# Last stage of a transformer layer: weight rows one chunk further ahead on GpSimd and ScalarE, and the residual of half of the tiles added on VectorE

## The chip, the cores and the metric

The kernel runs on one core of a Trainium2 chip. Times are device microseconds (us) of one execution. The core has five engines that run their own instruction streams side by side: TensorE (PE, with its weight loads as PEld), VectorE (DVE), ScalarE (ACT), GpSimd (POOL) and SyncE (SP, which here issues transfers). They are tied together by semaphores alone: an instruction may wait until a counter has reached a number, and may raise a counter when it is done.

## The reference, cut to what matters

One layer over 32 x 256 = 8192 tokens of width 128: windowed attention with 16 heads, residual and layer norm, then a mixture of 8 experts of which each token takes two, residual and layer norm. The change lies in the very last part:

```
combine = zeros((t, e)).at[arange(t)[:, None], top_idx].add(top_w)
y   = einsum('tef,efd->ted', h, w2) + b2
out = einsum('ted,te->td', y, combine)         # two weighted rows per token
x   = _layernorm(x + out, axis=-1)             # (x - mean) / sqrt(var + 1e-5)
```

So each token's result is the layer norm of residual + w0 * z0 + w1 * z1, where z0 and z1 are the rows that its two experts gave.

## The kernel before

Three stages follow one another: attention with the routing (its last score matmul starts at 387.3 us), the experts (71 steps of 256 tokens; their last scatter is issued at 694.5 us), and the last stage, which begins when the last expert rows have been scattered to the DRAM tensor zs and takes the rest. Only this last stage is touched.

It works through 64 tiles of 128 tokens in 16 chunks of 4 tiles (`CHUNKS = 16`, `CH = 4`). For chunk c:

- SP loads both expert rows of its tokens (512 KB) from zs into one of 6 buffers of `zin` (line 567). The load of chunk c+6 waits for the sum of chunk c, and stands in SP's order behind the store of chunk c-1.
- POOL multiplies the second rows by their weights, one instruction of 128x512 (line 654). I call it z1(c).
- ACT multiplies the first rows of the first two tiles (`ZA = 2`, line 815), z0a(c). DVE does the last two (line 1143), z0b(c).
- PE adds up in one PSUM bank of four (`total(c)`), each time with the identity as weights: the residual Y (line 1375), z1 (line 1377), z0 (line 1380). PE waits for z1(c), z0a(c) and z0b(c), and for the output of chunk c-4, whose bank it takes. The end of the third matmul raises `sum_full`, which I call sum(c).
- DVE takes the statistics of the sum (bn_stats, line 1150), joins them (line 1155) and writes the variance plus epsilon (line 1159), which I call var2(c).
- POOL raises that to the power -0.5, pow(c) (line 660).
- DVE makes minus mean times that (line 1165), nmr(c).
- ACT writes the normalized output, four instructions, yout(c) (line 823), and SP stores it, 256 KB (line 572).

Nothing plans the order: it is written out by loops. In round c of its loop each engine works on chunk c and then on an older one:

- POOL: z1(c), then pow(c-1)
- ACT: z0a(c), then yout(c-2)
- DVE: z0b(c), then bn_stats, join and var2 of c-1, then nmr(c-2)
- PE: Y(c), z1(c), z0(c)

An engine runs its instructions strictly in this order, so what stands behind a wait is late too. The intermediate values (`MBUFS = 3`) and the outputs (`YBUFS = 3`) have three buffers each.

Of the kernel before, what the change touches and what calls it, by code (L numbers as in the profile page):

```python
# [7 lines left out]
ALU = mybir.AluOpType  # L8
# [4 lines left out]
B, S, D = 32, 256, 128  # L13
# [43 lines left out]
CH = 4  # L57
# [3 lines left out]
CHUNKS = TILES // CH  # L61
ZBUFS, YBUFS, MBUFS, ZA = 6, 3, 3, 2
# [51 lines left out]
def build(nc, x, xT_in_dram, wq, wk, wv, wo, bq, bk, bv, bo, gate_w, w1, b1, w2, b2, c_ident, c_kmask, c_qhot, c_tri, c_tab, out):  # L114
# [3 lines left out]
    with ctx:  # L118
        def sb(name, shape, dt=FP32):
            return ctx.enter_context(nc.sbuf_tensor(name, shape, dt))  # L120
# [8 lines left out]
        ident = sb("ident", [P, P])  # L129
# [20 lines left out]
        Y = sb("Y", [P, TILES, YW])  # L150
# [13 lines left out]
        def late(words, pattern, dt=FP32, **sizes):  # L164
            a = area[:, taken[0]:taken[0] + words]
            taken[0] += words
            return (a if dt == FP32 else a.bitcast(dt)).rearrange(pattern, **sizes)
# [49 lines left out]
        wts = sb("wts", [P, TILES, TOPK])  # L217
# [16 lines left out]
        zin = late(ZBUFS * TOPK * CH * D, "p (b k n d) -> p b k n d", b=ZBUFS, k=TOPK, n=CH)  # L234
# [113 lines left out]
        sum_full = sem("sum_full")  # L348
# [51 lines left out]
        def total(c):  # L400
            return (pS, pT)[c % 4 // 2][:, c % 2, :]
# [180 lines left out]
        @block.gpsimd  # L582
        def _(pool):
            pool.memset(ones_row[:, :], 1.0).then_inc(zeroed, 1)
            pool.memset(neg_half[:, :], -0.5).then_inc(zeroed, 1)
            pool.memset(eps[:, :], EPS).then_inc(zeroed, 1)
            pool.memset(padrow[:, :, :], 0.0).then_inc(zeroed, 1)
            pool.wait_ge(zeroed, 4)
            pool.memset(padrow[:, :, C_ID:C_ID + 1], NOWHERE).then_inc(zeroed, 1)
            pool.memset(v_nat[:, :, :, :], 1.0).then_inc(v_ones, 1)  # L590
            pool.memset(VB[:, :, :, :, :], 0.0).then_inc(vb_zero, 1)
            pool.memset(b2h, 0.0).then_inc(b2_zero, 1)
            pool.memset(b2raw[:, :, :], 0.0).then_inc(b2_zero, 1)

            pool.wait_ge(b2_zero, 2)
            pool.memset(area[MR:P, KM_WORDS // 2:], 0.0).then_inc(km_zero[1], 1)
            pool.wait_ge(km_zero[1], 1)
            pool.wait_ge(qhot_in, 16)
            for gh in range(GH):
                nc.gpsimd.tensor_copy(*hot_groups(1, gh, gh + 1)).then_inc(masks_odd_pool, 1)  # L600
                pool.wait_ge(masks_odd_pool, gh + 1)
            pool.wait_ge(kmask_in, 16)
            for n in range(4):
                h = H - 4 + n
                nc.gpsimd.tensor_copy(*mask_heads(1, h, h + 1)).then_inc(masks_odd_pool, 1)
                pool.wait_ge(masks_odd_pool, GH + n + 1)

            def root_of(k):
                t0, size = BATCHES[k]
                reach(pool, mv_done, t0 + size)  # L610
                nc.gpsimd.tensor_tensor(var_eps[:, k % 2, 0:size], mv[:, t0:t0 + size, 1], view(eps[:, :], [[0, size]]), ALU.add).then_inc(var_done, 1)
                reach(pool, var_done, k + 1)
                nc.gpsimd.tensor_tensor(rstd[:, t0:t0 + size], var_eps[:, k % 2, 0:size], view(neg_half[:, :], [[0, size]]), ALU.pow).then_inc(rstd_done, 1)

            def dispatch(t, k, s):
                reach(pool, pos_done, k + 1)
                reach(pool, y_done, t + 1)
                for c in range(TOPK):
                    if live(s):
                        reach(pool, scores_full, 2 * s + c + 1)  # L620
                    nc.gpsimd.indirect_dma_start(xs, bass.IndirectOffsetOnAxis(ap=pos[:, c, t:t + 1], axis=0),  # L621
                                                 Y[:, t, 0:ROW], None).then_inc(rows_out[t % BODY], 16)

            def roots(s, hurry):
                for k in range(len(BATCHES)):
                    if ready(k) == s and urgent(k) == hurry:
                        root_of(k)

            for s in range(LAST):
                roots(s, True)  # L630
                for k, (t0, size) in enumerate(BATCHES):
                    for n in range(size):
                        if ranked(k) + 1 + n == s:
                            dispatch(t0 + n, k, s)
                roots(s, False)

            def scatter(j):
                if in_steps(j):
                    u, v = j % DBUFS, j % ZROWS


                    reach(pool, dst_done, j + 1)
                    reach(pool, z_done, j + 1)
                    for n in range(NH):
                        nc.gpsimd.indirect_dma_start(zs, bass.IndirectOffsetOnAxis(ap=dst[:, u, n:n + 1], axis=0), zrow[:, v, n, :], None,  # L645
                                                     bounds_check=TOPK * TOKENS - 1, oob_is_err=False).then_inc(zs_out[v], 16)
            expert_steps(scatter)


            for c in range(CHUNKS + 1):  # L650
                if in_chunks(c):
                    u = c % ZBUFS
                    reach(pool, z_in[u], 16 * (c // ZBUFS + 1))
                    nc.gpsimd.tensor_tensor(zin[:, u, 1, :, :], zin[:, u, 1, :, :], view(wts[:, c * CH:(c + 1) * CH, 1], [[TOPK, CH], [0, D]]),  # L654
                                            ALU.mult).then_inc(z1_done, 1)
                g = c - 1
                if in_chunks(g):
                    reach(pool, var2_done, g + 1)
                    reach(pool, yout_done, g - MBUFS + 1)
                    nc.gpsimd.tensor_tensor(rstd2[:, g % MBUFS, :], var2[:, g % MBUFS, :], view(neg_half[:, :], [[0, CH]]), ALU.pow).then_inc(rstd2_done, 1)  # L660

        @block.scalar
        def _(act):
# [143 lines left out]
                    last.then_inc(gelu_done, 1)  # L807
            expert_steps(expert)

            for c in range(CHUNKS + 2):  # L810
                if in_chunks(c):
                    u = c % ZBUFS
                    reach(act, z_in[u], 16 * (c // ZBUFS + 1))
                    for n in range(ZA):
                        last = nc.scalar.activation(zin[:, u, 0, n, :], zin[:, u, 0, n, :], ACT.Identity, scale=wts[:, c * CH + n, 0:1])
                    last.then_inc(z0a_done, 1)
                g = c - 2
                if in_chunks(g):
                    w, v = g % YBUFS, g % MBUFS
                    reach(act, nmr2_done, g + 1)  # L820
                    reach(act, yout_out[w], 16 * (g // YBUFS))
                    for n in range(CH):
                        last = nc.scalar.activation(yout[:, w, n, :], total(g)[:, n * D:(n + 1) * D], ACT.Identity,
                                                    scale=rstd2[:, v, n:n + 1], bias=nmr2[:, v, n:n + 1])
                    last.then_inc(yout_done, 1)

        @block.vector
        def _(dve):
# [184 lines left out]
            for s in range(FIRST, LAST):  # L1013
# [25 lines left out]
                for k, (t0, size) in enumerate(BATCHES):  # L1039
# [13 lines left out]
                    n = (s - chosen(k)) * per  # L1053
# [84 lines left out]
            for c in range(CHUNKS + 2):  # L1138
                if in_chunks(c):
                    u = c % ZBUFS  # L1140
                    reach(dve, z_in[u], 16 * (c // ZBUFS + 1))
                    for n in range(ZA, CH):
                        last = nc.vector.tensor_scalar(zin[:, u, 0, n, :], zin[:, u, 0, n, :], wts[:, c * CH + n, 0:1], None, ALU.mult)
                    last.then_inc(z0b_done, 1)
                g = c - 1
                if in_chunks(g):
                    v = g % MBUFS
                    reach(dve, sum_full, g + 1)
                    for n in range(CH):
                        last = nc.vector.bn_stats(st2[:, v, n, :], total(g)[:, n * D:(n + 1) * D])  # L1150
# [3 lines left out]
                    for n in range(CH):  # L1154
                        last = nc.vector.bn_aggr(mv2[:, v, n, :], st2[:, v, n, :])
# [4 lines left out]
                g = c - 2  # L1160
                if in_chunks(g):
# [4 lines left out]
                                                   op0=ALU.mult, op1=ALU.mult).then_inc(nmr2_done, 1)  # L1166

        @block.tensor
        def _(pe):
# [202 lines left out]
            for c in range(CHUNKS):  # L1372
                u = c % ZBUFS
                reach(pe, yout_done, c - 3)
                nc.tensor.matmul(total(c), ident[:, :], Y[:, c * CH:(c + 1) * CH, 0:D], start=True, stop=False)
                reach(pe, z1_done, c + 1)
                nc.tensor.matmul(total(c), ident[:, :], zin[:, u, 1, :, :], start=False, stop=False)
                reach(pe, z0a_done, c + 1)
                reach(pe, z0b_done, c + 1)
                nc.tensor.matmul(total(c), ident[:, :], zin[:, u, 0, :, :], start=False, stop=True).then_inc(sum_full, 1)  # L1380


def constants():
# [44 lines left out]
```

## Time and profile before

| | us |
|---|---|
| median of 3 runs | 759.72 (759.15 to 766.87) |
| the profiled execution: its own time | 757.98 |
| the profiled execution: its span | 756.2 |
| PE busy over the span | 605.1 (80%) |
| DVE busy | 505.0 (67%) |
| ACT busy | 391.3 (52%) |
| POOL busy | 349.7 (46%) |

A chain of waits starts from the last instruction and goes back to whatever released it. A line of the timeline gives when a group of instructions starts, how long it is under way, the engine, the line of the code, what it writes and reads and how many instructions it holds; in brackets is how long the engine had been idle and what ended that. The mean of a group in the view by line is the time from the start to the end of one instruction; when instructions follow each other closely they overlap, and the next starts before the one before has ended. All buffers of the last stage lie in one tensor named `area`; Y holds the residual, `wts` the weights, pS and pT are the four PSUM banks of the sums.

### The profile page before, as it was taken

The page shows a single profiled execution, that of the slowest core. Times are in us where ns is not written, and L with a number is a line of the kernel's source. Part 1 is how long each engine was busy: PE and PEld are TensorE (multiplying, and loading weights), DVE is VectorE, ACT ScalarE, POOL GpSimd, SP SyncE. Part 2 cuts the span into 40 slices and gives each one's busy share as a digit, 9 for nine tenths or more (in the row PEclk, how much of TensorE's full clock was granted, in tenths as well). Part 3 has the DMA queues.
Part 4 walks back from the last instruction along what each step waited for, and adds up shares of the span by engine and source line. Part 5 has one row for each costly group of instructions (what it writes and reads, how often), then busy time and mean ns, then how long its engine had stood idle before and what let it go on. Part 6 is the DMA issues. An engine that isn't in the chain of part 4 may idle for free.

```text
span 756.2 us, 26507 instructions
## 1 busy us (share of the span) xinstructions
PE 605.1 (80%) x10228; PEld 436.7 (58%) x10228; DVE 505.0 (67%) x1574; ACT 391.3 (52%) x935; POOL 349.7 (46%) x364
## 2 busy tenths in 40 slices
PE   5889988888887888877772598888888888884895
PEld 3556655555555655544551487777777777783332
DVE  8668767767777757755647477667767676762664
ACT  3556645555655655534330464565555555552476
POOL 9101334434434434354436055554555555665574
PEclk9999999999999999968875699999999999997898
DMA  3986666776766666644212676666666666641794
GB/s 95 129 169 139 160 138 138 153 127 123 145 140 146 143 113 130 134 96 98 64 57 71 222 259 212 220 233 209 236 205 238 208 235 209 229 144 35 254 273 120
DMA packets 126818, 121.90 MB, mean 161 GB/s; under 512 B 46865, under 2 KB 105300, under 8 KB 126694
## 3 DMA queue, kind: packets, MB, share of 16 engines
q1 hardware_dynamic: 116374, 102.28, 52.0%
q0 software_dynamic: 8640, 17.06, 7.8%
q8 instruction: 82, 1.34, 0.8%
q10 hardware_dynamic: 1680, 0.87, 0.5%
q14 instruction: 42, 0.34, 0.2%
HBM read 40.68 MB, written 28.12 MB: 91 GB/s over the span
## 4 chain that ended last, share of the span: by engine, by line
PE 66%; issue 16%; DVE 5%; POOL 4%; DMA 3%; ACT 2%; SPq 2%; another core or an unknown queue 1%; ACTq 0%; POOLq 0%; DVEq 0%
PE pO L1367 13%; PE pT L1254 8%; PE pO L1273 8%; PE pT L1353 6%; PE pS L1353 6%; PE pS L1244 5%; PE pS L1260 4%; PE pC L1205 3%; PE pM L1284 2%; POOL area L654 2%; POOL area L660 2%; PE pC L1173 1%; DVE nmax L892 1%; PE pC L1174 1%; DMA xT<-xT_in_dram 1%
## 5 line engine op out<-in xcount | busy, mean ns | idle before, releaser
L645 POOL DMA_INDIRECT zs<-PT,dst x142 | 148.0, 1042 | 131.4 <-ACT PT L794 97.2
L621 POOL DMA_INDIRECT xs<-Y,pos x128 | 126.0, 984 | 172.5 <-PE pS L1244 124.1
L1367 PE MATMUL pO<-area,Q 128*128 128x128 f16 x1704 | 120.1, 220 | 28.5 <-issue 27.7
L734 ACT COPY PT<-pT 128x512 f32<-128x512 f32 x128 | 74.9, 586 | 104.7 <-PE pT L1254 98.5
L1367 PEld LDWEIGHTS pO<-area,Q 128*128 128x128 f16 x1704 | 103.0, 98 | 39.3 <-issue 37.5
L1273 PEld LDWEIGHTS pO<-VB,PT 128*32 128x32 f32 x4096 | 58.5, 114 | 79.8 <-issue 76.4
L1273 PE MATMUL pO<-VB,PT 128*32 128x18 f32 x4096 | 79.3, 190 | 30.7 <-issue 27.8
L892 DVE TENSOR_REDUCE nmax<-pS 128x8 bf16<-128x512 f32 x128 | 87.4, 683 | 7.8 <-PE pS L1244 7.6
L1254 PE MATMUL pT<-ident,E 128*128 128x128 f32 x512 | 89.7, 301 | 0.0
L1130 DVE SCALAR_TENSOR_TENSOR Q<-VB,Q 128x1024 f16<-128x1024 f32 x71 | 87.0, 1225 | 2.4
L1128 DVE TENSOR_SCALAR Q<-VB 128x1024 f16<-128x1024 f32 x71 | 54.2, 763 | 48.9 <-ACT VB L805 46.1
L740 ACT ACTIVATE E<-pS 128x512 f32<-128x512 f32 x128 | 76.8, 601 | 16.5 <-remote 10.4
L1254 PEld LDWEIGHTS pT<-ident,E 128*128 128x128 f32 x512 | 57.7, 148 | 14.3 <-issue 2.3
L1244 PE MATMUL pS<-area,Q 112*32 112x128 f16 x2048 | 56.2, 231 | 5.2 <-issue 4.0
L805 ACT ACTIVATE VB<-pT,area 128x256 f32<-128x256 f32 x140 | 56.6, 523 | 6.1 <-remote 4.2
L1260 PE MATMUL pS<-nmax,ident 128*128 128x512 bf16 x128 | 52.2, 407 | 8.7 <-DVE nmax L892 7.4
L787 ACT ACTIVATE xh<-pC 128x256 f16<-128x256 f32 x36 | 14.1, 391 | 86.6 <-remote 79.5
L805 ACT ACTIVATE VB<-pS,area 128x256 f32<-128x256 f32 x144 | 57.0, 497 | 1.5 <-PE pS L1353 1.3
L1353 PE MATMUL pS<-xh,area 128*128 128x256 f16 x288 | 55.6, 278 | 2.4 <-issue 2.0
L1353 PE MATMUL pT<-xh,area 128*128 128x256 f16 x280 | 52.6, 275 | 0.4 <-issue 0.4
L1244 PEld LDWEIGHTS pS<-area,Q 112*32 112x32 f16 x2048 | 32.2, 99 | 25.6 <-issue 19.5
L886 DVE TENSOR_TENSOR Y<-pM,Y 128x136 f32<-128x136 f32 x63 | 18.5, 293 | 39.6 <-PE pM L1295 18.2
(201 smaller groups left out, 1091.0 us busy)
## 6 DMA issues: line engine op xcount, KB each, us to landing
area<-wall SPq DMA_DIRECT2D x71, 546.0 KB
E<-xs SPq DMA_DIRECT2D x71, 132.0 KB
VB<-vwin SPq DMA_DIRECT2D x64, 144.0 KB
area<-zs SPq DMA_DIRECT2D x16, 512.0 KB, 4.3
area<-k_nat SPq DMA_DIRECT2D x90, 64.0 KB
Q<-q_nat SPq DMA_DIRECT2D x45, 128.0 KB
vwin<-v_nat SPq DMA_DIRECT2D x32, 144.0 KB
xT<-xT_in_dram SPq DMA_DIRECT2D x16, 256.0 KB
```

The lines of the kernel that those rows point to most:

```text
L621: nc.gpsimd.indirect_dma_start(xs, bass.IndirectOffsetOnAxis(ap=pos[:, c, t:t + 1], axis=0), Y[:, t, 0:ROW], None).then_inc(rows_out[t % B ...
L645: nc.gpsimd.indirect_dma_start(zs, bass.IndirectOffsetOnAxis(ap=dst[:, u, n:n + 1], axis=0), zrow[:, v, n, :], None, bounds_check=TOPK * T ...
L740: nc.scalar.activation(E[:, t % 2, a * 512:(a + 1) * 512], pS[:, a, :], ACT.Exp, scale=SCORE_SCALE).then_inc(exp_done, 1)
L805: last = nc.scalar.activation(G[:, w, c, :], bank[:, half, k * NT:(k + 1) * NT], ACT.Gelu, scale=1 / (UP * WUP), bias=b1_now[:, g % WBUFS, ...
L892: nc.vector.tensor_reduce(out=nmax[:, t % 2, a * HALF:(a + 1) * HALF], in_=pS[:, a, :].rearrange("p (h k) -> p h k", k=KEYS), axis=AX.X, o ...
L1130: nc.vector.scalar_tensor_tensor(out=flat(Hl, w), in0=flat(G, v), scalar=UP, in1=flat(Hh, w), op0=ALU.mult, op1=ALU.subtract).then_inc(hl_ ...
L1244: last = nc.tensor.matmul(pS[32 * j:32 * j + 32, a, n * GL * KEYS:(n + 1) * GL * KEYS], Q4[0:KC, g % 2, gh, c:c + WINDOW], KM[0:KC, g % 2, ...
L1254: last = nc.tensor.transpose(view(pT[:, a, :], [[P, NJ], [1, WINDOW]], hp * WINDOW), E[:, t % 2, k * P:(k + 1) * P], ident[:, :])
L1260: nc.tensor.matmul(pS[:, a, :], ident16[:, :], view(nmax[:, t % 2, a * HALF:(a + 1) * HALF], [[1, HALF], [0, KEYS]]), start=False, stop=Tr ...
L1273: last = nc.tensor.matmul(pO[32 * hp:32 * hp + 32, t % 2, (a * NJ + j) * OC:(a * NJ + j + 1) * OC], PT[:, t % 2, a, j, hp * WINDOW:(hp + 1 ...
L1353: last = nc.tensor.matmul(o, wts1[:, part, c * P:(c + 1) * P], xp[:, w, :], start=m == 0, stop=m == 2)
L1367: last = nc.tensor.matmul(o, hp[:, v, c, n * P:(n + 1) * P], wts2[:, part, c, :], start=False, stop=(c == FC - 1 and part == 0 and hp is Hl))
```

## The change

Three edits, all in the last stage.

1. POOL now does pow(c-2) in round c, where it did pow(c-1).
2. ACT now does yout(c-3) in round c, where it did yout(c-2).
3. DVE's two z0b instructions become scalar_tensor_tensor: they multiply by the weight and add the residual Y of the same tile. PE's residual matmul shrinks to the first two tiles (256 columns in place of 512) and now comes second: z1(c) over 512 columns starts the bank, Y over 256 columns follows, z0 over 512 columns ends it.

```
@@ -647,13 +647,13 @@
-            for c in range(CHUNKS + 1):
+            for c in range(CHUNKS + 2):
                 if in_chunks(c):
                     u = c % ZBUFS
                     reach(pool, z_in[u], 16 * (c // ZBUFS + 1))
                     nc.gpsimd.tensor_tensor(zin[:, u, 1, :, :], zin[:, u, 1, :, :], view(wts[:, c * CH:(c + 1) * CH, 1], [[TOPK, CH], [0, D]]),
                                             ALU.mult).then_inc(z1_done, 1)
-                g = c - 1
+                g = c - 2
...
@@ -807,14 +807,14 @@
-            for c in range(CHUNKS + 2):
+            for c in range(CHUNKS + 3):
...
-                g = c - 2
+                g = c - 3
...
@@ -1140,7 +1140,8 @@
                     for n in range(ZA, CH):
-                        last = nc.vector.tensor_scalar(zin[:, u, 0, n, :], zin[:, u, 0, n, :], wts[:, c * CH + n, 0:1], None, ALU.mult)
+                        last = nc.vector.scalar_tensor_tensor(out=zin[:, u, 0, n, :], in0=zin[:, u, 0, n, :], scalar=wts[:, c * CH + n, 0:1],
+                                                              in1=Y[:, c * CH + n, 0:D], op0=ALU.mult, op1=ALU.add)
@@ -1372,12 +1373,12 @@
                 reach(pe, yout_done, c - 3)
-                nc.tensor.matmul(total(c), ident[:, :], Y[:, c * CH:(c + 1) * CH, 0:D], start=True, stop=False)
                 reach(pe, z1_done, c + 1)
-                nc.tensor.matmul(total(c), ident[:, :], zin[:, u, 1, :, :], start=False, stop=False)
+                nc.tensor.matmul(total(c), ident[:, :], zin[:, u, 1, :, :], start=True, stop=False, skip_group_check=True)
+                nc.tensor.matmul(total(c)[:, 0:ZA * D], ident[:, :], Y[:, c * CH:c * CH + ZA, 0:D], start=False, stop=False, skip_group_check=True)
                 reach(pe, z0a_done, c + 1)
                 reach(pe, z0b_done, c + 1)
-                nc.tensor.matmul(total(c), ident[:, :], zin[:, u, 0, :, :], start=False, stop=True).then_inc(sum_full, 1)
+                nc.tensor.matmul(total(c), ident[:, :], zin[:, u, 0, :, :], start=False, stop=True, skip_group_check=True).then_inc(sum_full, 1)
```

How the instructions stand on POOL at the end of the program, before (the chunks 12 to 15; the names behind "waits" are the semaphores):

```order
L654 TENSOR_TENSOR area<-area,wts 128x512 [waits z_in_0]
L660 TENSOR_TENSOR area<-area,neg_half 128x4 [waits yout_done,var2_done]
L654 TENSOR_TENSOR area<-area,wts 128x512 [waits z_in_1]
L660 TENSOR_TENSOR area<-area,neg_half 128x4 [waits yout_done,var2_done]
L654 TENSOR_TENSOR area<-area,wts 128x512 [waits z_in_2]
L660 TENSOR_TENSOR area<-area,neg_half 128x4 [waits yout_done,var2_done]
L654 TENSOR_TENSOR area<-area,wts 128x512 [waits z_in_3]
L660 TENSOR_TENSOR area<-area,neg_half 128x4 [waits yout_done,var2_done] x2
```

and with the change:

```order
L654 TENSOR_TENSOR area<-area,wts 128x512 [waits z_in_0]
L660 TENSOR_TENSOR area<-area,neg_half 128x4 [waits yout_done,var2_done]
L654 TENSOR_TENSOR area<-area,wts 128x512 [waits z_in_1]
L660 TENSOR_TENSOR area<-area,neg_half 128x4 [waits yout_done,var2_done]
L654 TENSOR_TENSOR area<-area,wts 128x512 [waits z_in_2]
L660 TENSOR_TENSOR area<-area,neg_half 128x4 [waits yout_done,var2_done]
L654 TENSOR_TENSOR area<-area,wts 128x512 [waits z_in_3]
L660 TENSOR_TENSOR area<-area,neg_half 128x4 [waits yout_done,var2_done] x3
```

The two instructions still alternate, but three powers stand behind the last z1 where there were two: each z1 has moved ahead of one more power.

PE at two neighbouring chunks, before:

```order
L1375 MATMUL pS<-Y,ident 128x512 [waits yout_done]
L1377 MATMUL pS<-area,ident 128x512 [waits z1_done]
L1380 MATMUL pS<-area,ident 128x512 [waits z0b_done,z0a_done]
L1375 MATMUL pT<-Y,ident 128x512 [waits yout_done]
L1377 MATMUL pT<-area,ident 128x512 [waits z1_done]
L1380 MATMUL pT<-area,ident 128x512 [waits z0b_done,z0a_done]
```

and with the change:

```order
L1377 MATMUL pS<-area,ident 128x512 [waits z1_done,yout_done]
L1378 MATMUL pS<-Y,ident 128x256
L1381 MATMUL pS<-area,ident 128x512 [waits z0b_done,z0a_done]
L1377 MATMUL pT<-area,ident 128x512 [waits z1_done,yout_done]
L1378 MATMUL pT<-Y,ident 128x256
L1381 MATMUL pT<-area,ident 128x512 [waits z0b_done,z0a_done]
```

The residual no longer comes first, ahead of the wait for z1; it comes behind it, and is half as wide.

## Rows read from the trace of the kernel before

**Rows 1.** The chain of waits, last stage: start us, us, what released the next.
```profile
716.13 1.05 POOL area L660
717.17 1.01 POOL area L654
718.19 0.48 issue
...
718.71 1.06 POOL area L660
```

**Rows 2.** Timeline: start us, us, engine, line, operation, operands, count [idle before <-releaser].
```profile
716.13 1.05 POOL L660 TENSOR_TENSOR area<-area,neg_half 128x4 f32<-128x4 f32 x1 [1.09 <-DVE area L1159]
717.15 1.04 POOL L654 TENSOR_TENSOR area<-area,wts 128x512 f32<-128x512 f32 x1
718.24 1.12 PE L1377 MATMUL pS<-area,ident 128*128 128x512 f32 x2 [0.30 <-POOL area L654]
719.20 1.02 PE L1380 MATMUL pS<-area,ident 128*128 128x512 f32 x2
720.06 1.02 PE L1375 MATMUL pT<-Y,ident 128*128 128x512 f32 x2
720.26 0.89 DVE L1150 BATCH_NORM_STATS2 area<-pS 128x6 f32<-128x128 f32 x4 [1.17 <-PE pS L1380]
720.92 1.03 PE L1377 MATMUL pT<-area,ident 128*128 128x512 f32 x2
721.19 0.38 DVE L1155 BATCH_NORM_AGGREGATE area<-area 128x2 f32<-128x6 f32 x4
721.60 0.17 DVE L1159 TENSOR_SCALAR area<-area 128x4 f32<-128x4 f32 x1
721.76 0.48 DVE L1143 TENSOR_SCALAR area<-area,wts 128x128 f32<-128x128 f32 x2
721.79 1.02 PE L1380 MATMUL pT<-area,ident 128*128 128x512 f32 x2
721.85 1.05 POOL L660 TENSOR_TENSOR area<-area,neg_half 128x4 f32<-128x4 f32 x1 [1.08 <-DVE area L1159]
```

**Rows 3.** By line and shape: busy us, mean ns of one, idle before and releasers.
```profile
L1143 DVE TENSOR_SCALAR area<-area,wts 128x128 f32<-128x128 f32 x24 | 5.7, 280 | 0.0
...
L930 DVE SCALAR_TENSOR_TENSOR w<-Wk,w 128x128 f16<-128x128 f32 x1 | 0.3, 299 | 1.7 <-ACT w L709 1.7
...
L930 DVE SCALAR_TENSOR_TENSOR w<-Wq,w 128x128 f16<-128x128 f32 x1 | 0.3, 279 | 0.0
```

**Rows 4.** Stretches: us; PE, PEld, DVE, ACT, POOL busy, PE clock, DMA share, GB/s.
```profile
701.00:706.00 5.00, 4.15 (x5) 1.85 (x6) 2.57 (x5) 1.69 (x6) 1.84 (x2) 0.50 1.05 398
716.00:722.00 6.00, 5.70 (x14) 2.30 (x13) 4.08 (x28) 4.29 (x13) 4.28 (x5) 1.00 0.95 277
740.00:746.00 6.00, 5.69 (x15) 2.15 (x13) 4.05 (x26) 4.43 (x14) 4.39 (x6) 1.00 0.31 87
```

**Rows 5.** DMA issues, 712 to 740 us: count, KB each, median us to landing.
```profile
area<-zs SPq DMA_DIRECT2D x9, 512.0 KB, 4.1
```

**Rows 6.** Timeline: load of chunk 7, and POOL at z1 of chunk 7.
```profile
712.38 0.51 SPq L567 DMA_DIRECT2D area<-zs  x1
722.88 1.04 POOL L654 TENSOR_TENSOR area<-area,wts 128x512 f32<-128x512 f32 x1
```

**Rows 7.** The chain of waits again, at the stage's start and end.
```profile
701.85 2.08 PE pS L1377 x2
703.92 1.71 PE pS L1380 x2
705.63 1.43 PE pS L1375 x2
707.06 0.86 PE pS L1377 x2
707.92 0.87 PE pS L1380 x2
...
748.03 0.87 PE pT L1380 x2
```

**Rows 8.** Line 1143 (z0b), 699 to 706 us: durations min/median/max.
```profile
L1143 DVE TENSOR_SCALAR area<-area,wts x4: 274/676/1169, 700.6 to 703.0; 128x128 f32<-128x128 f32 x4
```

**Rows 9.** Timeline: ACT at the end, both last outputs.
```profile
750.54 2.90 ACT L823 ACTIVATE area<-pT,area 128x128 f32<-128x128 f32 x8 [1.65 <-DVE area L1165]
```

## The prediction

> **What bounds the kernel now.** The change touches the last stage alone, so the question is what sets its pace of 16 chunks. I went first to the chain of waits. There POOL's power (line 660) and its weighting (line 654) take turns without another engine between them [rows 1]. That looks like a busy POOL, but the 0.48 us of "issue" between them is POOL waiting: the chain does not say for whom.
>
> The timeline says it [rows 2]. Follow one loop. pow starts at 716.13. z1 of the next chunk but one starts behind it at 717.15, 1.02 later, and takes 1.04. PE starts the matmul on that z1 at 718.24, and its sum is done just before bn_stats starts at 720.26. Then come bn_stats 0.89, the join at 721.19 and var2 at 721.60. At 721.85 POOL can start the pow of that chunk. The loop is 721.85 - 716.13 = 5.72 us long, and because POOL puts z1(c+1) behind pow(c-1), it advances by two chunks each turn: 2.86 us a chunk. It is a loop of latencies. No engine in it is full: over 6 us POOL is busy for 4.28, ACT 4.29, DVE 4.08, and PE for 5.70 [rows 4]. PE stands for 0.30 at the head of the loop [rows 2], and its three matmuls of 512 columns start 0.86 apart (719.20, 720.06, 720.92, 721.79), so it needs 3 x 0.86 = 2.58 of the 2.86.
>
> A count over the stage agrees. sum(1) is done at 707.92 + 0.87 = 708.79, sum(15) at 748.03 + 0.87 = 748.90 [rows 7]. Those 40.1 us for 14 chunks are 2.865 each.
>
> **The change, part by part.**
>
> POOL, one more chunk ahead. Now z1(c+1) stands behind pow(c-2). The same loop of 5.72 us, lengthened by Y, which now lies between z1 and z0 (0.43 at 256 columns, half of 0.86), is 6.1 us and advances by three chunks: 2.05 a chunk. It no longer sets the pace if an engine needs more.
>
> PE, 2.5 matmuls in place of 3. At 0.86 for 512 columns that is 2.15 us a chunk. Its clock stays at 1.00 of full, 2.4 GHz, since PE has fewer gaps than now. The narrow matmul's weight load must hide under a pass half as long; the trace has no such row. Below, that costs nothing. Above, I allow 0.1 a chunk, and take 0.05.
>
> The other engines, each against 2.15. POOL: a pow starts 1.02 before the z1 behind it, which takes 1.04: 2.06, plus a few hundredths to take up the next wait, 2.1. ACT: eight outputs take 2.90 [rows 9], so about 0.35 each; six instructions a chunk are at most 2.1. DVE: from bn_stats at 720.26 to the end of z0b at 721.76 + 0.48 = 722.24 are 1.98 [rows 2]. The new z0b instruction is not in the trace with these operands. It took 279 and 299 ns with 128 columns elsewhere, z0b before takes 280 [rows 3]: 0 to 0.04 more for two. DVE 2.0. So four engines lie between 2.0 and 2.15, PE on top. I take **2.2 us a chunk**, between 2.15 (nothing collides) and 2.3.
>
> ACT's shift. yout(c) now waits in ACT's order behind z0a(c+3) and no longer behind z0a(c+2). Its input nmr(c) follows var2(c+1), about 1.5 us behind sum(c+1) (720.26 to 721.77 [rows 2]), and z0a(c+3) is weighted by then. The loop through ACT is yout 1.4, z0a 0.7, z0 on PE 0.86, bn_stats to var2 1.5, pow 1.05 and up to 1.5 until DVE comes to nmr: 7.0 over four chunks, 1.8 a chunk. Priced at nothing. What covers it is that nmr, and not ACT, is late; if ACT had over 2.15 us of work, this would no longer hold. The wait of pow(c) for yout(c-3) stays satisfied, since yout(c-3) starts nearly two chunks before it.
>
> The start. PE runs at half clock there, 0.50 [rows 4]. Y(0) had been done long before. Now it lies between z1(0) and z0(0): 701.85 + 2.08 + half of 1.71 + 1.71 = 706.5 for sum(0), in place of 705.63 [rows 7]. Chunk 1 needs about 2.2 behind it, where it needed 1.43 + 0.86 + 0.87. sum(1) comes at 708.7, as now: nothing gained or lost. z1(2) is done by then, because it no longer waits for pow(0).
>
> The end. Behind sum(15) come bn_stats, var2, pow, nmr, yout(14), yout(15) and a store, in the same order: 7.3 us of span as now.
>
> Transfers. This is what a faster pace runs into. Chunk 7 is loaded at 712.38 and used at 722.88 [rows 6]; the load lands after 4.1 [rows 5], so 6.4 us are to spare. With the change sum(4) is at 708.7 + 3 x 2.2 = 715.3, pow(4) 1.6 behind it, z1(7) 1.0 behind that: 717.9. The load, released by yout(0), which does not move, lands at 712.4 + 4.1 = 716.5: 1.4 to spare. z1(7) would end at 718.95 and PE take it at sum(6), 719.7: another 0.7. Two us in all. How much a chunk costs the DMA is bounded from both sides. A load alone moves 398 GB/s at a share of 1.05, so 524 KB take 1.38 us at a share of 1; a store alone moves 87 GB/s at 0.31, so 262 KB take 0.93 [rows 4]. Their sum, 2.3, is the lower end. Mixed, they move 277 GB/s at a share of 0.95: 786 KB take 2.7, the upper end. Against 2.2 the loads fall behind by 0.1 to 0.5 a chunk over the 8 loads that follow: 0.8 to 4, of which 2 are covered. The cost is 0 to 2, and I take 0.5.
>
> **The sum.** 14 chunks take 14 x 2.2 = 30.8 in place of 40.1: -9.3. Start -0.1, end 0, transfers +0.5. Total -8.9 us. The span goes from 756.2 to 747.3, the profiled execution's own time from 757.98 to 749.1. That execution stood 1.7 under the median of the runs; I take the saving from the median: 759.72 - 8.9 = **750.8 us**. With 2.15 and free transfers it would be 749.5.
>
> **The rivals.**
>
> *The engines hinder each other on the way to 2.15* (chance 0.12). POOL would be busy nearly without a pause. If var2, a small DVE instruction in SBUF, cannot run beside z1, POOL's round becomes z1 + var2 with its signals (0.25, from 721.60 to 721.85) + pow = 2.35. 14 x 2.32 to 2.35 is 32.7: 7.4 saved, 752.3 us. For it: pow must follow var2 at once in such a round. Against: in the rows nothing of DVE is stretched beside POOL once the stage runs.
>
> *Transfers become the bound* (0.12). If the 2 us of slack are not there, nine chunks run at 2.7: 9 x 0.5 = 4.5 of the gain goes, 4.9 to 5.1 stay, 754.7. For it: the share of 0.95 now. Against: the two alone add up to 2.3.
>
> *DVE waits for POOL.* The first four z0b took 274 to 1169 ns while POOL weighted its first chunks [rows 8], up to 0.89 more than the 280 of later ones [rows 3]. Later z0b ran beside pow alone, and POOL was idle just before. If one of the two z0b of a chunk pays 0.89, DVE's round is 1.98 + 0.89 = 2.87, just what the loop takes now: 759.7, no change (0.07). If both pay, it is 3.76, 14 x 3.76 = 52.6 in place of 40.1: **12.5 slower, 772.2** (0.09). It decides from 0.89 of waiting a chunk on. For it: POOL will be busy 2.1 of 2.2 us, and the new instruction reads a second tensor from SBUF. Against: z0b follows var2 directly, so it starts beside pow (721.76 against 721.85), which ran beside it at 0.48 for two. Its place does not change unless POOL is late.
>
> The Trainium skill speaks for this rival: "SBUF — State Buffer", section "Who interferes with whom", says that a VectorE instruction with two SBUF inputs contends with a GpSimd instruction that reads SBUF, and that whoever issues first holds the shared ports for the whole of its instruction. By that rule each z0b would wait for a whole pow or z1 whenever POOL came first, which is the case of both paying, 772.2. The trace does not yet show an instruction with two SBUF tensors beside pow.
>
> *The change does not shorten the loop.* Some other wait could tie z1(c+1) to pow(c-1) still. The order shows none on POOL: z1 waits for its load alone. I give it no chance of its own.
>
> **The numbers.** The forecast has 0.60. A measurement of this kernel tells about 1% from no change, 7.6 us, so faster means below 752.1. Forecast 0.60, less 0.04 for its slow edge, and half of the first rival give 0.62 faster. The other half, the transfers, the single wait and that edge give 0.29 to 0.30 the same. Slower 0.08 to 0.09. The range goes from the fast end of the forecast with the lowest of the runs, 749.5 - 0.6, to past the case of the transfers, 756.5; it leaves out the two cases of the ports.
>
> **What would show it.** In the profile after, PE's matmuls of lines 1377 to 1381 should run without gaps, with sum to sum 2.15 to 2.25 us, and POOL should wait some hundredths before pow. z0b should stay near 280 to 300 ns; if it shows 600 or more, the ports decide. If z1, z0a or z0b wait for their load after chunk 9, transfers decide. I am wrong if the distance from sum(1) to sum(15) is over 33 us, or if the start or the end of the stage moves by more than 1 us.

## The result, and the profile after

| | before | after |
|---|---|---|
| median of the runs, us | 759.43 (758.61 to 766.87, 4 runs) | 751.34 (750.18 to 752.26, 4 runs) |
| ratio of the comparison | | 0.986 (0.9819 to 0.9902) |
| span of the profiled execution | 756.2 | 750.5 |
| first load of the last stage issued at | 696.70 | 699.88 |
| last stage, from there to the end of the span | 59.5 | 50.6 |

The change makes the kernel faster. The median lies 0.5 us above the forecast of 750.8. The ratio, taken on the 759.43 of before, gives 748.8, a tenth below the range's low end of 748.9. So two readings of the same runs fall on either side of the range's edge: the medians lie 8.1 us apart, the ratio says 10.6, and one of the four runs of before, 766.87, lies 7 us above the other three. The last stage alone, which the change touches, gave 8.9 us. All ratios here are taken over runs less than 1.5% above the fastest of their kernel; the profiled execution of the changed kernel's third comparison is not one of them, but its last stage is as long as in the others.

The chain of waits of the changed kernel now runs through PE, matmul behind matmul, through nearly the whole stage (start us, us, engine, bank, line, count; "..." marks what is left out):

```profile
705.10 2.08 PE pS L1377 x2
707.17 0.85 PE pS L1378 x2
708.02 1.71 PE pS L1381 x2
709.73 1.35 PE pS L1377 x2
711.08 0.43 PE pS L1378 x2
711.51 0.86 PE pS L1381 x2
...
720.96 0.86 PE pT L1377 x2
721.82 0.43 PE pT L1378 x2
722.25 0.86 PE pT L1381 x2
723.11 0.94 PE pT L1377 x2
...
742.32 0.87 PE pT L1381 x2
```

Set against [rows 7]: sum(1) is at 711.51 + 0.86 = 712.37, sum(15) at 742.32 + 0.87 = 743.19. The 14 chunks take 30.8 us in place of 40.1. The narrow matmul costs half of a wide one, 0.43. But from chunk 7 on (723.11) the matmul on z1 is 0.94 long and no longer 0.86: PE is waiting there, and sum to sum takes 2.23 in place of 2.15. Its cause stands in the timeline of the changed kernel (chosen lines, columns as in [rows 2]):

```profile
720.59 0.60 DVE L1143 SCALAR_TENSOR_TENSOR area<-area,wts,Y 128x128 f32<-128x128 f32 x2
720.68 1.11 POOL L660 TENSOR_TENSOR area<-area,neg_half 128x4 f32<-128x4 f32 x1
721.77 1.04 POOL L654 TENSOR_TENSOR area<-area,wts 128x512 f32<-128x512 f32 x1
722.03 0.38 DVE L1156 BATCH_NORM_AGGREGATE area<-area 128x2 f32<-128x6 f32 x4
722.45 0.39 DVE L1160 TENSOR_SCALAR area<-area 128x4 f32<-128x4 f32 x1
722.75 0.15 DVE L1166 SCALAR_TENSOR_TENSOR area<-area 128x4 f32<-128x4 f32 x1
722.82 0.60 DVE L1143 SCALAR_TENSOR_TENSOR area<-area,wts,Y 128x128 f32<-128x128 f32 x2
722.91 1.11 POOL L660 TENSOR_TENSOR area<-area,neg_half 128x4 f32<-128x4 f32 x1
```

Compare with [rows 2]. var2 (line 1160) starts at 722.45 while z1 runs, and ends at 722.84, just behind the end of z1 at 722.81; it takes 0.39 where it took 0.17. Then pow can start, at 722.91. POOL's round is 1.09 (pow to z1) + 1.04 + 0.10 (end of z1 to pow) = 2.23, more than PE's 2.15. All four compute engines are now nearly full, as the stretches of the changed kernel show (columns as in [rows 4]):

```profile
716.00:722.00 6.00, 6.00 (x18) 3.07 (x17) 5.86 (x32) 5.56 (x17) 5.68 (x7) 1.00 0.83 237
722.00:728.00 6.00, 6.00 (x18) 2.75 (x17) 5.80 (x33) 5.55 (x17) 5.68 (x6) 1.00 1.08 367
```

In the second stretch the transfers move 367 GB/s, loads and stores mixed, where the same mix moved 277 at a share of 0.95 before.

### The profile page after: what moved, and what is told of

Its sections match the earlier page's. It is cut to its first block, busy times and chain, and to the rows that moved or that the text cites. A ratio compares the mean times of both kernels' runs of the same rounds, so it can differ in the third digit from the quotient of the medians.

```text
span 750.5 us, 26519 instructions
## 1 busy us (share of the span) xinstructions
PE 594.7 (79%) x10228; PEld 435.7 (58%) x10228; DVE 508.0 (68%) x1574; ACT 391.6 (52%) x935; POOL 348.3 (46%) x364
## 4 chain that ended last, share of the span: by engine, by line
PE 71%; issue 14%; DVE 5%; ACT 3%; DMA 2%; another core or an unknown queue 2%; SPq 2%; POOL 0%; ACTq 0%; DVEq 0%; POOLq 0%
PE pO L1368 14%; PE pT L1255 8%; PE pO L1274 8%; PE pS L1354 7%; PE pT L1354 6%; PE pS L1245 5%; PE pS L1261 4%; PE pC L1206 3%; PE pM L1285 2%; PE pC L1174 1%; DVE nmax L892 1%; DMA xT<-xT_in_dram 1%; PE pS L1377 1%; PE pC L1175 1%
## 5 line engine op out<-in xcount | busy, mean ns | idle before, releaser
L1274 PE MATMUL pO<-VB,PT 128*32 128x18 f32 x4096 | 77.2, 189 | 35.8 <-issue 31.5
L1274 PEld LDWEIGHTS pO<-VB,PT 128*32 128x32 f32 x4096 | 55.8, 114 | 77.4 <-issue 72.7
L1128 DVE TENSOR_SCALAR Q<-VB 128x1024 f16<-128x1024 f32 x71 | 54.7, 771 | 54.2 <-ACT VB L805 50.6
```

Source lines behind the costliest of these rows:

```text
L1274: last = nc.tensor.matmul(pO[32 * hp:32 * hp + 32, t % 2, (a * NJ + j) * OC:(a * NJ + j + 1) * OC], PT[:, t % 2, a, j, hp * WINDOW:(hp + 1 ...
```

## The experiments

Each variant is a small edit of the changed kernel or of the one before. The table gives what the profile of each shows of the last stage: from the first load issued to bn_stats(0), from bn_stats(1) to bn_stats(15), the mean of a chunk in that, and the stage in all. The stage repeats within 0.6 us between executions (changed kernel 50.6, 50.1, 50.2; before 59.5, 60.0). The times of whole runs do not, though no variant changes anything ahead of the last stage but for one memset (with the reduce). On the first chips the first load was issued at 695.8 to 699.9 us in the profiles of the kernel before and of the changed one. On another chip it was issued at 579.4 to 589.1, for the changed kernel 114 to 118 us earlier than in its first profile. There the traces say where the spread of 9.7 us arises: the last score matmul of the attention ends between 327.4 and 337.4, while the experts, from the first to the last matmul on the tile xh, take 209.4 to 210.6 us in all eight profiles. In the first pair it is another place: the last matmul on xh ends at 684.3 and 683.7, the last scatter is issued at 694.5 and 697.6, and in the changed kernel's trace that scatter and the one before it stand behind an instruction on ACT (line 794) that had waited 6.9 us for something the profile does not name.

The variants with POOL put back, with the reduce, with no var2, with z0b as before and with Y first alone were executed once, for their profile, so they have a stage and no ratio.

| kernel | to bn_stats(0) | (1) to (15) | a chunk | stage |
|---|---|---|---|---|
| before | 8.97 | 40.10 | 2.864 | 59.5 |
| changed | 9.89 | 30.80 | 2.200 | 50.6 |
| shifts of POOL and ACT alone | 9.03 | 36.05 | 2.575 | 55.6 |
| residual edit alone | 9.54 | 44.05 | 3.146 | 63.0 |
| changed, POOL put back | 9.53 | 44.04 | 3.146 | 63.0 |
| changed, ACT put back | 9.59 | 34.43 | 2.459 | 53.7 |
| changed, var2 by a reduce | 9.68 | 30.12 | 2.151 | 49.9 |
| changed, no var2 | 9.67 | 30.30 | 2.164 | 49.8 |
| changed, z0b as before | 9.58 | 30.46 | 2.176 | 49.5 |
| changed, Y first | 9.09 | 31.22 | 2.230 | 49.8 |
| changed, Y first and reduce | 8.77 | 30.42 | 2.173 | 48.9 |

**The whole, and its parts.**

> The changed kernel itself once more, to size the whole step in the same rounds as its parts. In the profiles the last stage (first load issued to the end of the span) went from 59.5 to 50.6 us, so 8.9 us or 1.2% is expected; if the stage explains only a part, the ratio could be 0.986 as in the first comparison, 10.6 us.

Measured: 0.9929 (0.989 to 0.9968), stage 50.1. The stage came out as expected, the whole run did not. On a median of 644.86 us the ratio stands for 4.6 us, and the 8.9 of the stage would be 0.986 there (not the 1.2% of the expectation, which is their share of 759), outside the interval.

```
-                g = c - 1            # POOL, line 656, on the kernel before
+                g = c - 2
-                g = c - 2            # ACT, line 817
+                g = c - 3
```

> POOL and ACT one chunk further ahead, PE and DVE as before (residual wholly on PE, first). Theory: the two-chunk loop of 5.72 us is gone, and PE with three matmuls of 512 columns is next, 2.58 us a chunk: 14 x (2.865 - 2.58) = 4.0 us faster than before, half of the change. Rival, the narrower PE work is what counts: no gain here. Rival, POOL sets the pace alone: 2.23 a chunk here too, 8.9 faster.

Measured: 0.9932 (0.9882 to 0.9982), 2.575 a chunk where 2.58 was expected. PE's three matmuls are the pace. The loop no longer holds up POOL's z1, and PE's matmuls start 0.86 apart without a pause (chosen lines):

```profile
613.75 1.02 PE L1375 MATMUL pS<-Y,ident 128*128 128x512 f32 x2
614.00 1.04 POOL L654 TENSOR_TENSOR area<-area,wts 128x512 f32<-128x512 f32 x1
614.61 1.02 PE L1377 MATMUL pS<-area,ident 128*128 128x512 f32 x2
615.47 1.02 PE L1380 MATMUL pS<-area,ident 128*128 128x512 f32 x2
615.55 1.05 POOL L660 TENSOR_TENSOR area<-area,neg_half 128x4 f32<-128x4 f32 x1 [0.51 <-DVE area L1159]
616.33 1.02 PE L1375 MATMUL pT<-Y,ident 128*128 128x512 f32 x2
```

> DVE adds half of the residual and PE has 2.5 matmuls with z1 first, POOL and ACT as before. Theory: the loop still ties z1(c+1) to pow(c-1), and the 0.43 us of the narrow residual matmul now lie within it: 6.15 / 2 = 3.08 a chunk, 14 x 0.21 = 3 us slower than before. Rival, PE's work is the bound: 14 x 0.43 = 6 us faster.

Measured: 1.0096 (1.0056 to 1.0135), 3.146 a chunk. Alone, the edit that takes work from PE makes the kernel slower, 3.5 us in the stage. The chain of waits of that variant has the same turn-taking of POOL as [rows 1]. Its gaps are 1.89 and 0.07, together 1.96:

```profile
606.88 1.12 POOL area L660
608.00 1.01 POOL area L654
609.01 1.89 issue
...
610.93 1.13 POOL area L660
612.06 1.01 POOL area L654
613.07 0.07 issue
...
613.18 1.12 POOL area L660
```

Before, they were 0.48 ([rows 1]) and, one chunk earlier, 1.05, together 1.53:

```profile
715.04 1.05 issue
```

The difference is the 0.43 of Y. The loop from pow to pow is 613.18 - 606.88 = 6.30: 5.72, the 0.43 of Y now inside it, and 0.15 more. The timeline puts that 0.15 in two places: z1 starts 1.10 behind pow where it started 1.02 behind it, and PE starts 0.14 behind the end of z1 where it started 0.05 behind it.

```
-                g = c - 2            # POOL, on the changed kernel
+                g = c - 1
```

> The changed kernel with POOL as before (pow(c-1) in round c) and ACT left one chunk further ahead. Theory: POOL's place alone makes the loop, so the pace is that of the variant with neither shift, 3.15 us a chunk, 44 us from bn_stats(1) to bn_stats(15). Rival: ACT's shift carries part of it, and the pace lies under 3.

Measured: 3.146 a chunk, the same as with neither shift. POOL's place alone makes the loop; ACT's shift carries no part of it.

```
-                g = c - 3            # ACT, on the changed kernel
+                g = c - 2
```

> The changed kernel with ACT as before (yout(c-2) in round c). Theory: z0a(c+1) stands behind yout(c-2) again, which waits for nmr(c-2), at the end of DVE's round c: sum(c-1) + 1.6 + 1.4 + 0.7 = 3.7 for z0a(c+1), and with z0 0.86 behind it sum(c+1) comes 4.6 behind sum(c-1): 2.3 a chunk in place of 2.23, about 1 us slower than the changed kernel. Rival, as priced in the prediction, ACT's shift is worth nothing: same time as the changed kernel.

Measured: 0.9969 (0.993 to 1.0009), 2.459 a chunk. The mechanism is the expected one, its price was too low: 2.46 a chunk and not 2.3, so 3.6 us and not 1. In its timeline z0a (line 815) stands behind yout (line 823), and PE's z0 waits for it, in this chunk and in the next:

```profile
614.82 1.50 ACT L823 ACTIVATE area<-pS,area 128x128 f32<-128x128 f32 x4 [0.17 <-DVE area L1166]
616.21 0.70 ACT L815 ACTIVATE area<-area,wts 128x128 f32<-128x128 f32 x2
616.96 0.30 PEld L1381 LDWEIGHTS pS<-area,ident 128*128 128x128 f32 x2 [0.23 <-ACT area L815]
...
619.63 0.30 PEld L1381 LDWEIGHTS pS<-area,ident 128*128 128x128 f32 x2 [0.67 <-ACT area L815]
```

**What makes 2.23 out of 2.15.**

```
-   nc.vector.tensor_scalar(var2[:, v, :], mv2[:, v, :, 1], EPS, None, ALU.add)
+   nc.vector.tensor_reduce(out=var2[:, v, :], in_=mv2[:, v, :, 1:3], axis=AX.X, op=ALU.add)
```

(mv2 has a tensor of its own here, with a third column that holds epsilon. So the place of the data changes with the operation; the move alone was not run.)

> The changed kernel with var2 made another way: epsilon lies in a third column beside mean and variance, and a tensor_reduce adds the two columns. Theory: in the changed kernel var2 (0.39 us where it was 0.17) stands still until z1 of POOL has ended, because a tensor_scalar between two places in SBUF uses what POOL holds, and pow can only then follow: 1.09 + 1.04 + 0.10 = 2.23. The reduce does not wait, so the pace falls to PE's 2.15, bn_stats(1) to bn_stats(15) from 30.8 to 30.1. Rival, var2 is late for another reason (DVE's own order): 2.23 stays.

Measured: 2.151 a chunk, 30.12. The reduce takes 161 to 163 ns in all 13 rows of the stretch, the tensor_scalar 389 in the median. First the changed kernel, var2:

```profile
L1160 DVE TENSOR_SCALAR area<-area x13: 170/389/392, 715.9 to 742.5; 128x4 f32<-128x4 f32 x13
```

then the variant (durations in ns, min/median/max):

```profile
L1162 DVE TENSOR_REDUCE area<-mv x13: 161/161/163, 712.3 to 738.1; 128x4 f32<-128x8 f32 x13
```

> The changed kernel without var2: epsilon is left out, POOL takes the power of the variance that the join wrote. Theory: nothing on DVE that POOL waits for can be held by z1, so POOL runs pow and z1 back to back, 1.09 + 1.04 = 2.13, and PE's 2.15 is the pace; 30.1 from bn_stats(1) to bn_stats(15). Rival, the join is held by z1 just as var2 was: 2.23 or more stays.

Measured: 2.164 a chunk, 30.30, with one z1 that waited 0.54 for its load. The four joins that POOL now waits for stay at 149 ns in the median (183 at most), though z1 runs beside them: they are not held. Nor is the reduce. The tensor_scalar is. The two variants differ in how they take the held instruction away, and both reach PE's pace, so the cause is shown: var2 behind z1 makes PE wait.

```
-   nc.vector.scalar_tensor_tensor(..., in1=Y[:, c * CH + n, 0:D], op0=ALU.mult, op1=ALU.add)
+   nc.vector.tensor_scalar(zin[:, u, 0, n, :], zin[:, u, 0, n, :], wts[:, c * CH + n, 0:1], None, ALU.mult)
```

> The changed kernel with z0b as the old multiplication, so the residual of half of the tiles is left out. In the changed kernel z0b takes 0.60 for two where it took 0.48, and the pow beside it 1.11 where it took 1.05. Theory: the instruction with two inputs in SBUF and pow hold each other up for 0.06 to 0.12; without it pow is 1.05 again, POOL's round 1.02 + 1.04 + 0.10 = 2.16, and the pace 2.15 to 2.17. Rival, the longer pow comes from POOL being nearly full: 1.11 and 2.23 stay.

Measured: 2.176 a chunk (2.15 to 2.17 but for one chunk whose z1 waited 0.29 for its load). This variant leaves the residual of half of the tiles out. pow falls back to 1.05, which puts the 0.06 on the two-input z0b beside pow. The changed kernel:

```profile
L660 POOL TENSOR_TENSOR area<-area,neg_half x13: 1111/1112/1114, 714.0 to 740.7; 128x4 f32<-128x4 f32 x13
```

and with the old z0b:

```profile
L660 POOL TENSOR_TENSOR area<-area,neg_half x13: 1044/1046/1047, 702.8 to 729.2; 128x4 f32<-128x4 f32 x13
```

But var2 is held here as well:

```profile
L1159 DVE TENSOR_SCALAR area<-area x13: 170/383/722, 702.6 to 728.7; 128x4 f32<-128x4 f32 x13
```

So the 2.23 has two parts, and either one taken away is enough. With var2 held and a short pow, POOL's round is 1.02 + 1.04 + 0.10 = 2.16; with the long pow and nothing held, PE's 2.15 is the limit.

**Going further, and the spread.**

```
+   nc.tensor.matmul(total(c)[:, 0:ZA * D], ident[:, :], Y[...], start=True, ...)
    reach(pe, z1_done, c + 1)
-   nc.tensor.matmul(total(c), ident[:, :], zin[:, u, 1, :, :], start=True, ...)
-   nc.tensor.matmul(total(c)[:, 0:ZA * D], ident[:, :], Y[...], start=False, ...)
+   nc.tensor.matmul(total(c), ident[:, :], zin[:, u, 1, :, :], start=False, ...)
```

> The changed kernel with the narrow residual matmul ahead of the wait for z1 as its only difference. Theory: 9.8 to 9.9 us from the first load to bn_stats(0) become 9.0, as in the kernel before; the pace of 2.23, set by POOL and var2, stays, so about 0.5 to 0.9 us in all. Rival: PE's order at the start does not matter, because the loads or DVE end last there: no gain.

Measured: 9.09 to bn_stats(0), as expected, but 31.22 from bn_stats(1) to bn_stats(15), 0.4 more. Two loads came late (POOL's timeline):

```profile
604.87 1.04 POOL L654 TENSOR_TENSOR area<-area,wts 128x512 f32<-128x512 f32 x1 [0.28 <-DMA area<-zs]
606.02 1.11 POOL L660 TENSOR_TENSOR area<-area,neg_half 128x4 f32<-128x4 f32 x1
607.86 1.07 POOL L654 TENSOR_TENSOR area<-area,wts 128x512 f32<-128x512 f32 x1 [0.73 <-DMA area<-zs]
```

The second of them costs more than its own wait. z1 now starts just ahead of z0b (607.86 and 607.95), and DVE's first z0b of that chunk takes 1.14 where it takes 0.34 elsewhere, 1.40 for the two:

```profile
607.95 1.40 DVE L1143 SCALAR_TENSOR_TENSOR area<-area,wts,Y 128x128 f32<-128x128 f32 x2
```

Of the 0.8 us gained at the start, 0.2 to 0.8 remain in the stage.

> The changed kernel with var2 by the reduce, and with the narrow residual matmul ahead of the wait for z1 again. Theory: the reduce takes the pace to 2.15 (28 to 30 ns less for each chunk than 2.20, 0.7 us in all), and Y(0) no longer lies between z1(0) and z0(0) while PE runs at half clock, which gives 0.85 us at the start: 48.9 to 49.2 in the stage, some 1.5 us under the changed kernel. Rival, loads are then late (z1 waited once for a load in the variants that ran at 2.15): the gain stops at 0.7.

Measured: 0.9885 (0.9824 to 0.9945), stage 48.9, 1.1 to 1.7 under the changed kernel in the profiles, the lowest of all versions. (The step from 2.20 to 2.15 is 50 ns a chunk and not 28 to 30; the 0.7 us is right.) The changed kernel was run again beside it:

> The changed kernel a third time, beside the version that goes further. Stage 50.1 to 50.6 us in the profile, 9 to 10 us under the 59.5 to 60.0 of before, so a ratio of 0.988 if the stage is all; the control strayed by 0.2% from itself, so 0.985 to 0.991 would still be the same effect.

Measured: 0.9841 (0.978 to 0.9902), stage 50.2. The intervals overlap, so the whole runs do not tell the two apart.

> The kernel before, unchanged, timed against itself, and profiled on the chip of the parts. Its last stage (first load issued to the end) should be 59.5 us as in the first profile, against 50.1 for the changed kernel on that chip, and the ratio 1.000. If the ratio of a kernel against itself strays by some tenths of a per cent, the distance between the 8.9 us that the stage gave and the 10.6 us of the first ratio needs no cause in the change; if it stands within 0.2% of one, the change would have to act outside the last stage.

Measured: 0.9978 (0.9946 to 1.0009), stage 60.0. The kernel before against itself strays by 0.2%, 1.7 us; its twelve times go from 749.69 to 757.67. That lies right on the border that the expectation drew, and the interval holds one, so the control decides little. The changed kernel's three ratios against the same code before, 0.986, 0.9929 and 0.9841, say more: 10.6, 4.6 and 10.2 us for a stage that gave 8.9 to 10.0.

## Why the prediction was right or wrong, point by point

- **The loop.** Right. pow, z1, PE and DVE tied two chunks together, and POOL's place alone did it: put back, 3.15 a chunk. That Y now lies inside the loop, 0.43, was right too; it shows only where the loop still binds.
- **14 chunks in 30.8.** Measured 30.8, 30.9 and 30.8, but that is luck in good part. 2.2 was made of PE's 2.15 and 0.05 for the narrow matmul's weight load. That load costs nothing: 0.43 is half of 0.86. The 30.8 is made of 5 chunks at 2.15 and 9 at 2.23. The excess is the first rival's mechanism, smaller than priced: once var2 is only held, and not put behind z1 whole, it costs 0.10 behind z1's end and not 0.25, and pow is 0.06 longer. 2.23, where the rival had 2.35: 0.7 us over PE's pace in all, where the rival had 2.6. That "nothing of DVE is stretched beside POOL" was true of the rows because var2 did not run beside z1 there: POOL was idle ([rows 2]).
- **DVE.** z0b was priced at 0 to 0.04 more for two; it takes 0.60 for two where it took 0.48, 0.12 more. DVE is busy for nearly all of its round of 2.23, but 0.22 of it is the time that var2 is held. Its own work, about 2.0, stayed below PE's 2.15, so the longer z0b cost nothing on DVE.
- **DVE waits for POOL.** The 0.9 for each z0b did not come: 340 ns each in the steady part. The prediction's reason, that z0b starts just ahead of pow, is not enough. In 14 of the 16 chunks of the changed kernel the second z0b starts 0.09 to 0.17 us after pow has started, and takes 339 to 348 ns. Here is one, inside the pow of 722.91:

```profile
L1143 DVE SCALAR_TENSOR_TENSOR area<-area,wts,Y x1: 341/341/341, 723.1 to 723.1; 128x128 f32<-128x128 f32 x1
```

  What holds a z0b is z1. Where one starts in the first 0.2 us of a z1, it takes 1.13 to 1.16 us and ends 0.15 behind it: once at the start of the stage, and in both variants with Y first at a chunk whose load was late. The prediction's condition, that z0b keeps its place "unless POOL is late", was the right one. The Trainium skill ("SBUF — State Buffer", "Who interferes with whom") names tensor_scalar among the instructions that can take the ports that VectorE shares with GpSimd, and says that on trn2 tensor_reduce never contends. Both agree with the runs, 389 ns against 161 beside z1; the joins, 150 ns, were not held either. By the Trainium skill's rule for a VectorE instruction with two SBUF inputs 772 had been possible. It shows beside z1; beside pow all that shows is 0.06 us of a longer pow.
- **ACT's shift at nothing.** It cost nothing, as priced. But the prediction did not see that it is needed: without it 3.6 us are lost.
- **The start.** sum(0) came 0.9 later, as priced. From the first load to bn_stats(1) the changed kernel took 12.5, 11.9 and 12.1 us, the kernel before 12.1 and 12.7: no difference beyond the spread. **The end**: 7.3 and 7.3.
- **Transfers, +0.5.** Wrong. After the first three chunks no z1 waited for a load in the changed kernel's three profiles, so the term was 0. The upper end of 2.7 us a chunk took the share of 0.95 as full. The mix then moved 367 GB/s at a share of 1.08, so a chunk costs 0.786 MB / 367 GB/s = 2.14 us at most. That is still only just enough: z1(8) started 0.26 us after its load had landed, and of the variants that ran ahead by some tenths, four had a z1 that waited 0.3 to 0.8 for its load.
- **The sum.** In the first pair of profiles the parts are -9.3 for the 14 chunks, +0.4 for the start, 0 for the end and 0 for the transfers: 8.9 us, to the tenth what was forecast. Two errors, the +0.5 for transfers and the -0.1 for the start, cancelled.
- **The range's low end.** This is the step that failed. It was the forecast's fast case less 0.6, the distance of the lowest of three runs to their median. (The fast case is 749.6 by the prediction's own terms, 10.0 + 0.1 under 759.72, and not 749.5.) The stage did what was said, 8.9 to 10.0 us between the profiles. But a comparison of whole runs strays from its stage by far more than 0.6: the three comparisons of the changed kernel gave 10.6, 4.6 and 10.2 us. The mis-sized term is this allowance: 0.6 where the runs show 1.7 one way and 4.3 the other. That the ratio fell 0.1 us outside, and the median inside, is chance. The spread arises ahead of the last stage, in instructions that are the same; what makes them slower in one execution than in the next stays open.

## What to carry to other kernels

When two engines wait for each other across a pipeline, write down the loop and count by how many chunks its order advances: one more chunk of lead cut 2.86 to the next limit, while taking work from the engine that looked busiest made things worse until the loop was gone. When the loop is gone several limits lie close together, and small instructions that share something with a full engine set the rest. Judge a change of one stage by that stage's own profile: for a stage that gave 8.9 to 10.0 us, three comparisons of whole runs said 10.6, 4.6 and 10.2.

## What the runs showed of the hardware

- A tensor_scalar of 128x4 on VectorE beside a running GpSimd tensor_tensor of 128x512 took 389 ns and ended with it; with GpSimd idle 170. A tensor_reduce of 128x8 in the same place took 161, bn_aggr 149.
- A scalar_tensor_tensor of 128x128 with two SBUF inputs that started just behind that GpSimd instruction took 1130 to 1160 ns and ended 0.15 us behind it; just behind the start of a GpSimd pow of 128x4, itself 1.11 us long, it took 339 to 348 ns.
- An f32 matmul of 256 columns took 0.43 us, half of the 0.86 of one with 512, at the full clock, with its weight load hidden.
- Busy share of the DMA engines is no measure of what is left: 277 GB/s at 0.95 before, 367 GB/s at 1.08 after, with the same loads and stores.
- On one of the chips everything ahead of the changed kernel's last stage took 114 to 118 us less (first load at 581.6 and 585.9, against 699.9), while the last stage took 50.1 and 50.2 us, against 50.6.
